# New slots for every operation of a two-layer cross-attention and feed-forward kernel, and its first loads in another order

## The reference

```python
x = x + xattn0(norm(x), ctx, mask)      # 16 heads of 16, biases, mask==0 -> -1e9, softmax, W_o
x = x + ffn0(norm(x))                   # ternary weights: W/mean|W| rounded, clipped to -1..1; 256 -> 1024 relu -> 256
x = x + xattn1(norm(x), ctx, lens)      # 16 heads, keys at or beyond the length masked, W_o
x = x + ffn1(norm(x))                   # 8 small auto-encoders (256 -> 64 relu -> 256); for each sequence the one with the
                                        # least mean squared error names the adapter (256 -> 64 relu -> 256) that is added
                                        # to x @ W_base
```

## Time and profile before

| | |
|---|---|
| median of 3 runs | 1799.05 us (1795.69 to 1802.66) |
| the profiled execution | 1797.68 us, of which the span of instructions is 1795.7 us |
| PE busy | 1595.8 us, 89% |
| VectorE (DVE) busy | 1491.1 us, 83% |
| ScalarE (ACT) busy | 903.7 us, 50% |
| POOL busy | 977.2 us, 54% |
| mean granted TensorE clock | 0.969 |

### The profile page before, as it was taken

The page is one execution under the profiler, slowest core; times in us unless marked ns, Lnnn a source line. Parts: engine busy times, 40 slices in busy tenths (PEclk is TensorE's granted clock), DMA queues, the critical chain, the costliest instruction groups (busy, mean ns, idle before and its releaser), DMA issues.

```text
span 1795.7 us, 44012 instructions
## 1 busy us (share of the span) xinstructions
PE 1595.8 (89%) x15136; PEld 1290.6 (72%) x15136; DVE 1491.1 (83%) x5215; ACT 903.7 (50%) x2465; POOL 977.2 (54%) x1069
## 2 busy tenths in 40 slices
PE   2467999999999999999999999999999999999875
PEld 1355777787777777877777778777777787777654
DVE  2667798988889998888899998888899989888652
ACT  0123455555555555555555655555556555555542
POOL 2456655655565656555666565556665655564200
PEclk9879999999999999999999999999999999999987
DMA  6345456554554564555545655555546555542311
GB/s 172 57 65 91 87 85 105 93 90 93 96 84 85 92 105 93 90 93 95 88 79 94 105 98 85 93 99 90 77 89 105 97 90 89 99 83 50 57 35 30
DMA packets 286501, 157.32 MB, mean 88 GB/s; under 512 B 38964, under 2 KB 281928, under 8 KB 286280
## 3 DMA queue, kind: packets, MB, share of 16 engines
q1 hardware_dynamic: 286280, 154.51, 49.1%
HBM read 111.44 MB, written 41.96 MB: 85 GB/s over the span
## 4 chain that ended last, share of the span: by engine, by line
PE 52%; DVE 26%; issue 10%; DMA 5%; SPq 4%; POOL 2%; ACT 2%; POOLq 0%; DVEq 0%; ACTq 0%
PE psD L1182 7%; DVE dump L831 6%; PE psD L1214 5%; PE psD L1203 5%; PE psV L1170 4%; PE psD L1224 4%; PE psD L1118 4%; PE psD L1129 4%; PE psS L1143 4%; PE psX L1155 4%; DVE dif L902 3%; PE psD L1248 3%; DMA qs<-scr 2%; PE psD L1089 2%; DVE hhl L884 2%
## 5 line engine op out<-in xcount | busy, mean ns | idle before, releaser
L603 ACT ACTIVATE pT<-psX 128x512 f32<-128x512 f32 x512 | 305.4, 596 | 406.1 <-PE psX L1155 404.6
L506 POOL TENSOR_TENSOR pT<-pT,keep 128x512 f32<-128x512 f32 x256 | 334.5, 1312 | 94.3 <-ACT pT L603 86.9
L465 POOL TENSOR_SCALAR veps<-mv 128x2 f32<-128x2 f32 x128 | 28.9, 226 | 589.7 <-DVE mv L776 589.7
L491 POOL TENSOR_SCALAR xn<-xr,mv,rstd 128x256 f32<-128x256 f32 x256 | 312.1, 1226 | 7.3 <-POOL rstd L475 0.2
L831 DVE CUSTOM_DVE_ANT_0 dump<-psS,bias 128x128 bf16<-128x128 f32 x1024 | 234.3, 284 | 40.3 <-PE psS L1143 39.1
L823 DVE TENSOR_REDUCE mx<-psS 128x4 f32<-128x512 f32 x256 | 173.2, 677 | 102.5 <-PE psS L1143 100.7
L1143 PE MATMUL psS<-ks,qs 65*128 65x128 f16 x2048 | 204.4, 223 | 56.5 <-DMA qs<-scr 38.0
L647 ACT ACTIVATE dif<-dif 128x256 f32<-128x256 f32 x512 | 206.5, 408 | 75.6 <-DVE dif L902 75.4
L902 DVE SCALAR_TENSOR_TENSOR dif<-psD,bd2s,xT 128x256 f32<-128x256 f32 x512 | 213.1, 470 | 14.3 <-PE psD L1224 13.6
L1155 PE MATMUL psX<-qs,ks 67*128 67x128 f16 x2048 | 201.9, 221 | 20.0 <-ACT pT L603 15.5
L1143 PEld LDWEIGHTS psS<-ks,qs 65*128 65x128 f16 x2048 | 146.1, 99 | 99.1 <-issue 29.4
(11 more groups left out here) (101 smaller groups left out, 3177.1 us busy)
## 6 DMA issues: line engine op xcount, KB each, us to landing
scr<-packed SPq DMA_DIRECT2D x128, 256.0 KB, 2.8
ks<-scr SPq DMA_DIRECT2D x256, 128.0 KB, 4.5
qs<-scr SPq DMA_DIRECT2D x256, 128.0 KB, 4.6
adapter<-in_adapters SPq DMA_DIRECT2D x64, 192.5 KB, 2.7
xr<-in_x SPq DMA_DIRECT2D x32, 256.0 KB, 2.8
ctxT<-in_ctx SPq DMA_DIRECT2D x32, 256.0 KB, 3.1
qs<-mrows SPq DMA_DIRECT2D x512, 2.0 KB
out_y<-xr SPq DMA_DIRECT2D x32, 256.0 KB, 5.0
```

The costliest lines, as they stand in the source:

```text
L491: nc.gpsimd.tensor_scalar(xn[:, XN[s], b], xr[:, p % NX, b], mv[:, s, b, 0:1], rstd[:, s, b:b + 1], ALU.subtract, ALU.mult).then_inc(norme ...
L506: nc.gpsimd.tensor_tensor(blk, blk, keep[:, p % 2, j // 4].unsqueeze(1).to_broadcast([P, 4, P]), ALU.mult).then_inc(masked.sem, 1)
L603: nc.scalar.activation(pT[:, j % 4], X[:], ACT.Exp, scale=SCALE).then_inc(exp_done[l].sem, 1)
```

## The change

It has three parts.

1. **The start.** The feed-forward weights are loaded ahead of the lengths, pair 1 is loaded ahead of the slot loop, and the 15 LATE weights are issued one in each of slots -4 to 10. The nine broadcast DMAs go: two memsets, one on POOL and one on VectorE, write three whole partitions of `qs` and `ks` instead (6144 float32 elements in each partition). The sums for quantising move to slot -6 with the five small length operations behind them, the ten steps to slot -2, all at once.
2. **New slots and line orders** on all engines and on SP. `FIRST` goes from -14 to -16.
3. **Other banks** for the PSUM groups.

The core of the diff:

```diff
-FIRST = -14
+LATE_SLOT = -4
+GAMMA_SLOT = -6
+QUANT_SLOT = -2
+FIRST = -16
 BANKS = (
-    ("rec2", "cnt", "rec0", "rec7", "down", "up"),
-    ("rec4", "v0", "F1_1", "T2", "O1"),
-    ("O0", "k1", "T1", "rec5", "F2", "rec1", "loss"),
-    ("F1_3", "hd1", "rec3", "k0", "q1", "T3"),
-    ("q0", "v1", "T0", "rec6", "F1_0", "F1_2", "hd0"),
+    ("k1", "v0", "q1", "hd1"),
+    ("F1_3", "rec2", "down", "rec7", "loss", "hd0"),
+    ("O1", "rec3", "F1_1", "T2", "F2", "T1", "rec0", "F1_2"),
+    ("cnt", "rec5", "rec1", "q0", "O0", "F1_0", "T3"),
+    ("v1", "rec4", "T0", "rec6", "k0", "up"),
 )
...
+                sp.wait_ge(rows_set, 1)
+                sp.dma_start(const_dram, const_rows[:]).then_inc(len_stored, 16)
+                sp.dma_start(w1_ld..., rows(w1t)).then_inc(ffn_w_loaded, 16)
+                sp.dma_start(w2_ld..., rows(w2t)).then_inc(ffn_w_loaded, 16)
                 sp.dma_start(lens_c[:], ...)
                 sp.dma_start(lens_r[:], ...)
...
-                for n in range(NR):
-                    sp.dma_start(qs[MASK_ROW:MASK_ROW + 1, n], const_dram[1:2]...)
-                    for k in range(2):
-                        sp.dma_start(ks[MASK_ROW + 1 + k:MASK_ROW + 2 + k, n], const_dram[2:3]...)
+            load(1, True)
...
+                if LATE_SLOT <= t < LATE_SLOT + len(LATE):
+                    dst, src = LATE[t - LATE_SLOT]
+                        sp.dma_start(dst, src).then_inc(w_late, 16)
...
+            nc.gpsimd.memset(qs[MASK_ROW:MASK_ROW + 3]..., pair16(BIG16)).then_inc(q_rows_set, 1)
...
+            nc.vector.memset(ks[MASK_ROW:MASK_ROW + 3]..., pair16(M_UP)).then_inc(rows_set, 1)
...
-                if t == 0:
+                if t == GAMMA_SLOT:
+                    dve.wait_ge(ffn_w_loaded, 32)
...
-                if 2 <= t < 12:
-                    quantise(t - 2)
+                if t == QUANT_SLOT:
+                    for n in range(10):
+                        quantise(n)
```

More of the change, by code:

```diff
@@ L1 @@
+import struct
 from contextlib import ExitStack
@@ L311, in load @@
             def load(p, ahead=False):
-                if p == 0 and not ahead:
+                if p < 2 and not ahead:
                     return
@@ L417, in _ @@
                 for p in at(t, 43):
                     maxima(1, p, 0)
+                for p in at(t, 27):
+                    spill(1, 1, p)
                 for p in at(t, -4):
-                    spill(0, 0, p)
                     stack(0, 0, p)
-                for p in at(t, 29):
-                    spill(1, 1, p)
                 for p in at(t, 78):
                     store(p)
+                for p in at(t, 31):
+                    stack(1, 1, p)
+                for p in at(t, 47):
+                    maxima(1, p, 1)
@@ L427, in _ @@
+                if LATE_SLOT <= t < LATE_SLOT + len(LATE):
+                    dst, src = LATE[t - LATE_SLOT]
+                    with nc.allow_non_contiguous_dma(reason="biases, one or a few for each partition, once"):
+                        sp.dma_start(dst, src).then_inc(w_late, 16)
             for k in range(2):
@@ L955, in _ @@
                 for p in at(t, 16):
-                    turn_out(0, p, 1)
+                    scale_out(0, p, 1)
                 for p in at(t, 0):
                     maximum(0, p, 0)
-                for p in at(t, 16):
-                    scale_out(0, p, 1)
                 for p in at(t, 64):
@@ L973, in _ @@
                     differences(p, 4)
-                for p in at(t, 51):
-                    turn_out(1, p, 0)
                 for p in at(t, 3):
@@ L979, in _ @@
                     differences(p, 5)
-                for p in at(t, -13):
+                for p in at(t, 51):
+                    turn_out(1, p, 0)
+                for p in at(t, 4):
+                    split_max(0, p, 0)
+                for p in at(t, 36):
+                    low(1, 0, p)
+                for p in at(t, -12):
                     statistics(0, p)
@@ L1034, in _ @@
                     statistics(3, p)
-                for p in at(t, -5):
-                    low(0, 0, p)
                 for p in at(t, 43):
@@ L1051, in _ @@
                     statistics(2, p)
+                for p in at(t, 45):
+                    maximum(1, p, 5)
+                for p in at(t, 13):
+                    scale_out(0, p, 0)
+                for p in at(t, 78):
+                    add_up(p)
                 for p in at(t, 46):
@@ L1055, in _ @@
                     maximum(1, p, 7)
+                for p in at(t, 15):
+                    turn_out(0, p, 1)
+                for p in at(t, 47):
                     split_max(1, p, 1)
@@ L1258, in _ @@
                 for p in at(t, 48):
+                    scores_t(1, p, 2)
                     values(1, p)
@@ L1261, in _ @@
                     scores(0, p, 0)
-                for p in at(t, 48):
-                    scores_t(1, p, 2)
                 for p in at(t, 64):
@@ L1267, in _ @@
                     mix(1, p, 0)
-                for p in at(t, 33):
-                    turn(2, p)
+                for p in at(t, 49):
+                    scores_t(1, p, 3)
                 for p in at(t, 1):
@@ L1273, in _ @@
                     output(0, p)
-                for p in at(t, 49):
-                    scores_t(1, p, 3)
+                for p in at(t, 34):
+                    turn(2, p)
                 for p in at(t, 2):
                     scores(0, p, 2)
+                for p in at(t, 50):
+                    scores_t(1, p, 4)
                 for p in at(t, 66):
@@ L1288, in _ @@
                     queries(1, p)
+                for p in at(t, 67):
+                    reconstruct(p, 3)
+                for p in at(t, 19):
+                    turn(1, p)
                 for p in at(t, 4):
@@ L1368, in _ @@
                     scores_t(0, p, 7)
+                for p in at(t, 45):
+                    scores(1, p, 5)
                 for p in at(t, 61):
@@ L1377, in _ @@
                     hidden(p, 0)
+                for p in at(t, 46):
+                    scores(1, p, 6)
+                for p in at(t, 47):
+                    scores_t(1, p, 1)
                 for p in at(t, 63):
```

311 lines of the change are left out of this document (151 added, 160 removed).

## The result

| | before | after |
|---|---|---|
| median | 1797.37 us (4 runs) | 1732.66 us (4 runs, 1730.56 to 1735.72) |
| ratio | | 0.9628, 95% interval 0.9594 to 0.9661 |
| profiled execution / its span | 1797.68 / 1795.7 us | 1730.56 / 1728.6 us |
| first `add_ffn` | 131.76 us | 112.15 us |
| last `add_ffn` | 1692.33 us | 1625.02 us |

The kernel is 3.7% faster, about twice the forecast 32 us. The four `add_ffn` times split the 67.1 us between the two spans: 19.6 before the first one, 47.7 between the first and the last, and nothing behind (103.4 and 103.6 us). The start gave what was forecast; the pace moved by 1.92 us a pair, not 0.5.

A forecast was written before the change was run, and what follows sets the result against it. PE was taken to bound the kernel, with 48.7 us a pair its own work and 2.55 idle, and VectorE 90% busy. 1797.7 - 19 (start) - 13.5 (steady pairs) = 1765 us, range 1722 to 1832.

The forecast's parts named there:

- The start: Up to the first `scores`, near 38.5 instead of 52.93 us: 19 us won in all, between 9 and 27.
- What goes: PE's waits at `turn(0)`, `reconstruct(2)` and `output` in the steady cycle: 2.43 us a pair at most.
- The first two waits: `turn(0)` behind the ReLU of F1_2, 1.72 us a pair, and `reconstruct(2)` behind `add_att`, 0.41: both to go.
- what may come: New PE waits at tighter places in the steady cycle: 1.9 us a pair against 2.43 gone.
- Place 1: `turn(0)` and `output(1)`, behind VectorE's chain with its stands for POOL: 0.6 us of new wait (0 to 3.2).
- Place 2: `turn(1)`, waiting for the normed tokens: 0.3 us of new wait a pair (0 to 0.9).
- Place 3: `scores_t(1, 0)`, its maxima's DMAs now behind `spill(0, 0)` on SP: 0.5 us of new wait (0 to 1.7).
- what I couldn't lay out: `values(0)` behind `low(1, 0)` and `ffn_up(0)` behind `x_lows`, on a 90% full VectorE: 0.5 us (0 to 1.0).
- rival A: VectorE stays ahead, no lock before `output(1)`: new waits 0.7 us, 1.7 us a pair won; 1735 us, chance 0.22.
- 48.7 us a pair is PE's own work: Steady cycle: an order can win only PE's idle 2.55 us of the 51.21 a pair.
- B: Only the start wins; steady waits change place and keep their size: 1779 us, chance 0.20.
- C: Slower: four VectorE operations before `output(1)` each meet POOL, 2.5 us there, 4.8 in all; 1841 us, chance 0.26.

The follow-up runs named there:

- e1_start: The kernel before with the new start alone, old slots and old banks: 1777.17 us, ratio 0.9868.
- e3_bank: The kernel before with T0 alone moved from the bank of F1_2 to behind F1_1: 1807.68 us, ratio 1.0029.
- e5_shortmask_before: The kernel before with POOL's `apply_mask` cut to 8 of 128 tokens of each block: 1741.11 us, ratio 0.9684.
- x2_filler: The kernel before with the eight matmuls of `ffn_up(3)` issued twice, 0.9 us more PE work a pair: 1794.77 us, ratio 0.9972.
- e10_new_pe: The kernel before with PE's new order and the new banks alone: 1928.80 us, ratio 1.0715.

## Why the prediction was right and wrong

**The start: right, with some luck.** 19 us forecast, 19.6 measured at the first `add_ffn`; `scores` forecast at 38.5, measured at 38.26. In that second number two errors cancel. `low(0, 0)` began 1.5 us later than before (28.33 instead of 26.87), and from its spill to `scores` it took 9.2 us instead of 11.0. The two sums did not delay it: VectorE stood idle for 1.36 us in front of it, waiting for ScalarE. The delay begins on POOL, where `mask_bias` now stands ahead of the first norm, which began at 17.37 instead of 16.00:
```profile
15.75 1.54 POOL L476 TENSOR_SCALAR bias<-mqf,allc 128x128 f32<-128x128 f32 x2 [6.50 <-DVE allc L801]
17.37 0.23 POOL L482 TENSOR_SCALAR veps<-mv 128x2 f32<-128x2 f32 x1
```
The quantising took 8.4 us instead of 11. And the new start by itself is worth 24 us (`e1_start`); why 19.6 of them are left beside the new slots no run shows.

**What goes: right in size, its cause half seen.** The first two waits went; the third, at `output(1)`, which the forecast took out and reckoned anew, is now the largest. But I booked the 1.72 us at `turn(0)` to T0's bank. `e3_bank` shows that the bank alone wins nothing and `e5_shortmask_before` that the wait goes with the bank as it was: it came from the held operations, as I had written of it myself before I priced the change by banks.

**The steps that failed.** There are two, of about the same size. The pace moved by 1.92 us a pair and not by 0.53, so 1.39 are to be explained. Over 24 pairs PE was idle for 2.63 us a pair before and 1.32 after; it was busy for 48.58 before and 47.97 after. So 1.31 us came out of its waits, where 0.53 were forecast, and 0.61 out of its busy time, where the forecast had none.

**First, what may come.** "New waits: 0.6 + 0.3 + 0.5 + 0.5 = 1.9" measured 1.03 + 0.25 + 0 + 0 = 1.28.

- Place 1 was there, and dearer. PE's own work from `scores(0, 7)` to `output(1)` is 635.57 - 628.46 - 1.02 = 6.1 us (6.2 forecast). VectorE is late by one meeting, 1.1 us at L857, and a quarter of a microsecond at L881; the timeline of VectorE, POOL and PE in the changed kernel:
```profile
630.43 0.65 DVE L903 TENSOR_TENSOR hhl<-work,hhl 128x512 f16<-128x512 f32 x1
631.00 1.25 DVE L857 TENSOR_SCALAR m<-mx 128x16 f16<-128x16 f32 x1
...
634.28 0.66 DVE L881 TENSOR_TENSOR atok<-otok,rden 128x256 f32<-128x256 f32 x1
```
```profile
630.50 1.72 POOL L523 TENSOR_TENSOR pT<-pT,keep 128x512 f32<-128x512 f32 x1 [0.54 <-ACT pT L621]
```
```profile
628.46 0.39 PE L1167 MATMUL psS<-ks,qs 65*128 65x128 f16 x4
...
635.57 1.97 PE L1206 MATMUL psD<-wo,attT 128*128 128x256 f32 x8 [1.02 <-DVE attT L885]
```
- Place 2 was right: 0.25 for 0.3.
- Place 3, priced at 0.5, is 0. In the cycle shown, the four issues end at 648.88 us and PE uses them without a wait at 650.11: 1.2 us are enough where I had put 1.7.
```profile
646.24 2.64 SPq L377 DMA_DIRECT2D qs<-mrows  x4
```
```profile
650.11 0.40 PE L1179 MATMUL psX<-qs,ks 67*128 67x128 f16 x4
```
- The 0.5 for what I couldn't lay out is 0. It rested on "a VectorE that is 90% full", and VectorE is still 89% full. It does get back 2.0 us a pair that it had stood, a relief that the forecast never booked, though the earlier trace rows carry it; it was only in rival A. That this is why those places don't wait is my reading, and no run tests it.

The other 0.2 us are small waits that the earlier trace rows leave out: 2.63 us idle against the 2.43 named.

**Second, "48.7 us a pair is PE's own work".** The forecast took this as fixed and said that the idle 2.55 us were all that an order could win. The windows of single pairs show that it isn't fixed. The old pace of 51.21 is made of pairs of 50.8 us and of longer ones. Seven of the 24 have a granted clock of 0.97, and in these PE is busy for 49.4 to 49.8 us instead of 48.1 to 48.4. Three more wait up to 1.0 us in all for `q` by DMA. In the changed kernel all 24 pairs have 1.00 and most take 49.2. Two neighbouring pairs before, one pair after, one slowed pair of `x2_filler` (length, busy us of PE, PEld, DVE, ACT, POOL, clock):
```profile
528.39:580.12 51.73, 49.43 (x477) 40.43 (x481) 46.24 (x163) 28.08 (x78) 30.09 (x33) 0.97 0.52 92
580.12:630.95 50.83, 48.11 (x478) 39.43 (x481) 46.19 (x164) 28.22 (x78) 30.42 (x33) 1.00 0.54 93
```
```profile
599.48:648.72 49.24, 47.96 (x477) 39.04 (x475) 44.12 (x163) 28.00 (x77) 31.10 (x34) 1.00 0.54 96
```
```profile
679.47:731.93 52.46, 50.63 (x485) 41.14 (x488) 46.14 (x163) 28.21 (x78) 30.46 (x33) 0.97 0.53 90
```
In each of the seven the clock was at 0.50, the lower of its two levels (1.2 GHz), for 3.4 us, and each fall began within half a microsecond behind the end of PE's wait at `turn(0)`:
```profile
562.99 0.94 PE L1089 MATMUL psD<-ident,xn 128*128 128x128 f32 x4 [1.79 <-ACT work L627]
```
```profile
563.60:566.40 2.80, 2.80 (x28) 2.03 (x27) 2.52 (x4) 1.47 (x4) 0.97 (x2) 0.50 0.78 121
```
The seven account for (49.48 - 48.21) x 7 / 24 = 0.37 of the 0.61 us; the other 0.24, between 48.21 in the undisturbed pairs and 47.97 after, is not explained. The change took the wait at `turn(0)` away and the falls went from seven to none; `x2_filler` halved the wait, and four were left. Why seven of 24 such waits are followed by a fall and the others are not stays open, and a wait alone doesn't decide it: `e10_new_pe` waits up to 1.4 us at a time, and its windows of 250 us all show 1.00.

**Rivals.** A (1735) came nearest in number and pace (49.5), in part by luck: it wanted no meeting in place 1 and 0.7 us of new waits, there is one and they are 1.28, and PE's shorter busy time, which A did not have either, makes up the difference. B and C are out. C's mechanism, POOL without a pause in front of `output(1)`, is there but for one pause of 0.54 us, and costs 1.03 us where 2.5 were put, because only one of its four meetings happens in full.

## What to carry to other kernels

Before a wait is booked to the semaphore that ends it, ask what delayed the instruction that releases it: here PE waited for ScalarE, ScalarE for VectorE, and VectorE for POOL. Freeing the first link won nothing, shortening the last won 3%. When an order is changed to free one engine, book the relief where it arises as well as the new tight places. Don't take an engine's busy time as fixed before you have looked at it cycle by cycle, with its clock beside it. An order for several in-order queues stands or falls as a whole: VectorE's or PE's part of a change that wins 3% costs 7 or 8% by itself.

## What the runs showed of the hardware

A VectorE operation over 16 elements that meets a POOL operation costs up to 1.25 us instead of 0.13 (L857), and the POOL operation is lengthened in turn: 1.72 us instead of 1.27 for `apply_mask` where `h_lows` came first by 0.07 us (630.43 to 630.50). VectorE's transposes, reciprocals and `bn_stats` stood in neither trace: from 400 to 1400 us the least and the greatest time of each such line are at most 51 ns apart (394 and 445).

The quantising steps over 2048 float32 elements took 1.2 to 1.3 us each in the changed kernel; the same operations on the second weight took 1.41, 2.16 and 2.27 before, beside POOL's operations.
